# The reciprocal of the time mixer's denominator: a power of minus one on GpSimd in place of VectorE's reciprocal

## The reference

```python
def step(carry, kv):
    aa, bb, pp = carry
    kt, vt = kv
    ww = u + kt
    qq = jnp.maximum(pp, ww)
    e1 = jnp.exp(pp - qq)
    e2 = jnp.exp(ww - qq)
    out = (e1 * aa + e2 * vt) / (e1 * bb + e2)
    ...
    return ((e1 * aa + e2 * vt, e1 * bb + e2, qq2), out)
...
x = x + jnp.einsum('tbc,oc->tbo', r * wkv, Wo)
```

## Time and profile before

| what | us |
|---|---|
| median of 2 runs | 1938.91 (1937.6 to 1940.23) |
| the profiled execution, its own time | 1936.92 |
| its span, first to last instruction | 1935.2 |
| busy in the span: TensorE matmuls | 1686.4 (87%) |
| busy: VectorE | 1287.0 (67%) |
| busy: ScalarE | 864.3 (45%) |
| busy: GpSimd | 605.3 (31%) |

### The profile page before, as it was taken

How to read it: one execution, slowest core, us unless ns; L and a number is a source line. 1 busy time by engine, 2 the same in 40 slices (tenths; PEclk the granted TensorE clock), 3 DMA queues, 4 the chain that set the end, 5 groups by cost and what they waited for, 6 DMA issues and landing times.

```text
span 1935.2 us, 26723 instructions
## 1 busy us (share of the span) xinstructions
PE 1686.4 (87%) x8210; PEld 1308.0 (68%) x8210; DVE 1287.0 (67%) x4141; ACT 864.3 (45%) x1675; POOL 605.3 (31%) x984
## 2 busy tenths in 40 slices
PE   5899999992299999982779999999999999999775
PEld 3677777771166677761658778778778778777654
DVE  3567777762148777334478888889888889876642
ACT  1444444440031111114556766667766667754321
POOL 1111111213300000005534445545444544433211
PEclk9899999995699999995789999999999999999987
DMA  9000000006644343425000000000000000000000
GB/s 272 3 1 1 1 1 1 1 1 234 249 137 137 110 119 99 134 77 197 12 6 1 12 12 6 12 6 12 12 12 6 12 6 7 6 6 1 6 6 11
DMA packets 81573, 94.11 MB, mean 49 GB/s; under 512 B 19142, under 2 KB 69527, under 8 KB 81179
## 3 DMA queue, kind: packets, MB, share of 16 engines
q1 hardware_dynamic: 72747, 78.91, 12.7%
q0 software_dynamic: 3072, 8.39, 1.2%
q10 hardware_dynamic: 5616, 5.11, 0.8%
HBM read 71.94 MB, written 20.45 MB: 48 GB/s over the span
## 4 chain that ended last, share of the span: by engine, by line
PE 35%; DVE 13%; ACT 2%; issue 2%; POOL 2%; POOLq 0%; ACTq 0%
PE E_pY L2313 6%; PE E_pK L2204 5%; PE E_pU L2303 4%; PE E_pK L2163 3%; PE E_pY L2151 3%; PE E_pS L2266 3%; PE E_pY L2284 3%; PE E_pU L2275 2%; DVE E_wk L1738 2%; DVE E_ex L1670 2%; DVE E_m L1731 1%; PE E_pY L2163 1%; PE E_pT L2145 1%; DVE E_num L1677 1%; PE E_pY L2214 1%
## 5 line engine op out<-in xcount | busy, mean ns | idle before, releaser
L1222 ACT ACTIVATE F_uT<-F_puT 128x1024 f32<-128x1024 f32 x39 | 39.9, 1024 | 294.3 <-PE F_puT L1282 294.3
L1492 POOL TENSOR_SCALAR E_var<-E_mv 128x2 f32<-128x2 f32 x80 | 34.2, 427 | 355.9 <-DVE E_mv L1607 355.7
L1273 PE MATMUL F_pu<-C_W,F_hT 128*128 x312 | 143.9, 605 | 0.3 <-issue 0.3
L1291 PE MATMUL F_py<-C_W,F_uT 128*128 x624 | 141.2, 379 | 1.2 <-ACT F_uT L1222 1.2
L1291 PEld LDWEIGHTS F_py<-C_W,F_uT 128*128 128x128 f32 x624 | 115.6, 190 | 16.0 <-issue 1.9
L2214 PE MATMUL E_pY<-E_Wcv,E_hid 128*128 128x256 f32 x512 | 118.7, 386 | 3.3 <-issue 3.3
L2303 PE MATMUL E_pU<-E_xT,E_W 128*128 128x256 f32 x512 | 117.7, 385 | 2.3 <-ACT E_xT L2052 2.3
L2313 PE MATMUL E_pY<-E_W,E_hid 128*128 128x256 f32 x512 | 118.1, 379 | 0.0
L2204 PE MATMUL E_pK<-E_cmix,E_Wck 128*128 128x256 f32 x512 | 115.8, 379 | 1.3 <-ACT E_hid L1993 1.3
L2214 PEld LDWEIGHTS E_pY<-E_Wcv,E_hid 128*128 128x128 f32 x512 | 96.0, 192 | 27.8 <-issue 15.6
L2303 PEld LDWEIGHTS E_pU<-E_xT,E_W 128*128 128x128 f32 x512 | 98.7, 193 | 16.7 <-ACT E_xT L2052 2.9
(11 more groups left out here) (402 smaller groups left out, 4353.9 us busy)
## 6 DMA issues: line engine op xcount, KB each, us to landing
F_b<-in_L_ffn_b SPq DMA_DIRECT2D x39, 512.0 KB, 4.4
C_W<-in_L_ffn_W SPq DMA_DIRECT2D x16, 1024.0 KB, 14.0
sorted_x<-zero SPq DMA_DIRECT2D x1, 4992.0 KB, 19.5
F_xs<-sorted_x SPq DMA_DIRECT2D x39, 128.0 KB, 2.4
F_b<-in_L_ffn_b SPq DMA_DIRECT2D x39, 128.0 KB, 3.1
sorted_y<-F_y ACTq DMA_DIRECT2D x39, 128.0 KB, 2.3
out<-E_tB SPq DMA_DIRECT2D x16, 256.0 KB, 2.1
X<-in_x SPq DMA_DIRECT2D x3, 1024.0 KB, 10.7
```

Source lines behind the costliest of these rows:

```text
L1273: last = nc.tensor.matmul(p_u[:, f, :], hT[:, i % 2, kb, :], W1[:, bass.ds(e, 1), kb, f * 512:(f + 1) * 512], start=kb == 0, stop=kb == KD ...
L1291: last = nc.tensor.matmul(p_y[:, 0:D], uT[:, f, :], W2[:, bass.ds(e, 1), f, :], start=f == 0, stop=f == FB - 1)
```

## The change

`invert(t)` moves from VectorE's list to GpSimd's. There it stands right ahead of `state(t)` and computes `ex4[:, 0]` to the power -1 over the same 128 x 512 elements, in place, with a tile of one element a partition, broadcast, as the exponent. It waits for `den` and raises `inv`, as before. `gated(t)` on VectorE and its wait for `inv` are as they were. A memset of the exponent and one more wait stand in GpSimd's preamble.

```diff
+        minus_one = sb("minus_one", [P, 1])
...
         @block.gpsimd
...
+            def invert(t):
+                pool.wait_ge(d["den"], t + 1)
+                g.tensor_tensor(ex4[:, 0], ex4[:, 0], minus_one[:].unsqueeze(1).to_broadcast([P, KD, S]), ALU.pow).then_inc(d["inv"], 1)
...
+            g.memset(minus_one[:], -1.0).then_inc(step["masks"], 1)
             pool.wait_ge(d["init"], 5)
+            pool.wait_ge(step["masks"], 1)
...
-            pool.wait_ge(step["masks"], 1)
+            pool.wait_ge(step["masks"], 2)
...
                 if t < B:
+                    invert(t)
                     state(t)
...
         @block.vector
...
-            def invert(t):
-                dve.wait_ge(d["den"], t + 1)
-                v.reciprocal(ex4[:, 0], ex4[:, 0]).then_inc(d["inv"], 1)
...
                 if 0 <= p < B:
                     output(p)
-                if t < B:
-                    invert(t)
                 if 0 <= j < B:
                     take(j, 2)
                 if t < B:
                     gated(t)
```

## The result

The changed kernel takes 3205.26 us (median of 2 runs, 3204.97 to 3205.54) against 1938.91: a ratio of 1.654, with an interval of 1.650 to 1.658. The sign, the place and the mechanism were as forecast. The size was not: 1266 us more, where 1100 were predicted, and outside the stated range, which ended at 3110.

What follows compares the result with a forecast made beforehand. TensorE, fed closely by VectorE, was taken to bound the kernel. Delays of 69.0, 65.6 and 14 x 66.2 us (1061.4) plus 39 us of clock gave 1100 us more: 3039 us against the median, range 2440 to 3110.

Steps and rivals of the forecast that it cites:

- What bounds the kernel: Pipeline step of 57.9 us: TensorE follows VectorE with hardly a gap, so a shorter reciprocal yields only tenths of a us.
- When the power can start and who waits: Power starts on GpSimd at 1448.29; gated, all behind it on VectorE and TensorE's out_product wait, in every step.
- D = X - 5.9: Delay of gated in a full step, for a power of X us; 5.9 us is the break-even, 66.2 the forecast delay.
- the prediction's own sum for step 0: First step: 906.98 + 72.1 + 0.15 - 910.25 = 69.0 us of delay, with nothing behind which to hide.
- The duration: GpSimd's power of 512 elements: 568 + 511 x 140 ns = 72.1 us, at chance 0.75.
- The product behind the power: VectorE's gated, which waits for the power: the forecast held no term for a change in its length.
- The clock: TensorE's granted clock falls while it stands at out_product: 3 us a step in 13 steps, 39 us.
- What lies on GpSimd behind the power: State update and the rest of GpSimd's list come later, but are wanted late enough to cost nothing.
- Two or four elements side by side: Rivals on GpSimd's power: two at once 36.3 us, total 2465, chance 0.07; four 18.4 us, total 2178, chance 0.06.
- the dearer pairs: Rival on GpSimd's power: worked by pairs at 256 ns an element, 131.3 us, total 3985 us; chance 0.05.
- The streaming power: Rival: GpSimd's power costs what a product does, 1.3 us up to about 3; about 8 us less, 1929 us; chance 0.05.
- The stated signs: Expected in the changed profile: GpSimd about 58% busy, TensorE about 56%, a step every 127 us, VectorE idle 69.5 before gated.

Runs made afterwards that it cites:

- The ladder: Kernel before, with powers of 1 to 512 elements added alone in GpSimd's preamble of the last stage; a power of 512 took about 82.14 us, no kernel time given.
- the run with 177 products: Changed kernel plus 177 unread products a step on TensorE ahead of the waiting product, steps 3 to 15, so TensorE works while it would stand: 3175.35 us.

## Why the prediction was right or wrong

*What bounds the kernel* was right. A short operation in the power's place gave 12 us of VectorE's 53.6, which is the reading that TensorE follows VectorE with hardly a gap. The 8 us that I gave for it were too few.

*When the power can start and who waits* was right: D = X - 5.9 in full steps. With X at 81.9 it gives 76.0 us, and 75.9 were measured in the changed kernel's step. At half the length it holds too, and moving the power behind the state's update costs what the update lasts. Steps 0 and 1 have a break-even of about 3 us, as the prediction's own sum for step 0 implies; that made no difference at 81.9 us, but it did at 5.4.

*The duration* is the step that failed, and with it the range: the term X of the sum was too small. The prediction said "the one marginal cost that the rows show is for the very operation" and took 140 ns an element from the step between 1 and 2 elements. The ladder shows 144 ns there and 159.8 in a long power: 81.93 us in place of 72.1. Over 16 steps that is 16 x 9.83 = 157 us of the 166 that were missing. I had bounded the likeliest case by "2 us either way in X", for which no row stood. A slope from two points, extended 256-fold, deserved a range of its own: 15% of X either way would have held the result. Why the first elements are cheaper than the later ones stays open.

*The product behind the power* was taken as unchanged. It takes 1.75 us and not 0.95, since GpSimd's update starts at the same moment, and 0.69 where GpSimd idles (the run with the power behind the update): 0.8 x 16 = 13 us more.

*The clock* was right in kind and too dear: 3 us a step were taken, 2.2 measured by the run with 177 products, 10 us less in 13 steps. These three terms give 1100 + 157 + 13 - 10 = 1260, against 1268 in the two profiled spans (3203.3 - 1935.2). No run tests the last 8. By the two timelines, 1.5 had come before the mixer's first step, 6.5 lie in steps 2 and 3 and 3.5 behind the last out_product, and the other steps took 3.5 less than these terms. In step 3 the clock is part of it, which was costed only behind out_product: the next keys' product takes 3.78 us (at 1256.00) and 1.99 in the kernel before.

*What lies on GpSimd behind the power*, costed at nothing, held: the period is explained without it.

*The rivals.* Two or four elements side by side, and the dearer pairs, are refuted by the ladder. The streaming power would have given 1926 us, and its duration is refuted. The prediction took "about twice as slow there as on VectorE" for a case of it; twice the reciprocal's 3.35 us would be 6.7, already past the break-even, and the power took 24 times the reciprocal's time. The stated signs came out: GpSimd 60% busy (58 said), TensorE 54% (56), a period of 136.5 (127), a wait of 79.5 us a step before gated (69.5), each off by what X was off.

## What to carry to other kernels

Before work is shed onto an idle engine, ask who waits for the result and how soon: here 6 us were free in a full step and 3 in the first two, and everything above came back one for one in every step. A duration seen only on one or two elements gives the order of a long one's, and its range must be as wide as that extension is long; a power on GpSimd is no elementwise product. Busy shares did not show that the gain was capped at about 0.6% from the start. Part of the same slack, taken by moving finish up in VectorE's list, gave 0.27% without any other engine.

## What the runs showed of the hardware that was not expected

- A power on GpSimd costs 159.8 ns an element a partition in a long operation, for the two exponents and four bases tried, with a full tile of exponents or a broadcast one; a product of 512 elements takes 1.26 us there and the power 82.1, 65 times that. With one broadcast operand the product took 1.03. VectorE's reciprocal of the same elements took 3.35.
- VectorE's product of two SBUF tiles (128x512) took 1.75 us where one of GpSimd's operations of 128x512 started with it, 0.95 in the kernel before, where they overlapped otherwise, and 0.69 where GpSimd was idle; the same instruction did both 0.69 and 1.75 in one run. The Trainium skill, page "GPSIMD Engine Reference", section "Specifications", says that GpSimd's SBUF interfaces are shared with VectorE and that instructions with two SBUF inputs contend; the trace agrees.
- With the same gap of 2.8 us ahead of it, TensorE's waiting product took 1.97 us in one step and 3.65 in the next; with the gap nearly closed (0.64 us) it took 1.97 in every step.
